# A transformer layer on one core: all five engine orders planned anew, with costs taken from a trace

## The chip, the core and the metric

The kernel runs on one NeuronCore of a Trainium2 chip. The core has a matrix engine (TensorE, PE in the rows), VectorE (DVE), ScalarE (ACT), GpSimd (POOL), SyncE (SP, which here only issues transfers) and 16 DMA engines. The metric is device time in microseconds, from one execution to the next compared by the median. Before the change it is 617.42 us (median of 3 runs, 615.31 to 617.7).

## What is computed

Input is x of shape 4 x 1024 x 128 (four batches of 1024 tokens). One pre-norm layer follows:

```
x = x + attention(layernorm(x), W_attn, W_proj)
x = x + moe(layernorm(x), gate, bias, up, down, shared_up, shared_down)

attention:  q, k, v = x @ W_attn.T            # 16 heads of 8
            K, V = sums of k, v over the sets (0-3), (4-7), ..., (0-7), (8-15), ..., (0-1023)
            logits = q . K over the sets that end at or before t, and q . (sum of k over the set
                     of 4 that t stands in, up to t)
            out = softmax(logits) @ V, then @ W_proj.T
moe:        scores = sigmoid(x @ gate.T); 4 of 8 groups, then 6 of 32 experts per token
            sum over chosen experts of w * relu(x @ up_e.T)^2 @ down_e.T   # inner width 64
            + relu(x @ shared_up.T)^2 @ shared_down.T                       # inner width 256
```

All 32 experts are computed for all tokens and multiplied with a weight that is 0 for those not chosen.

## The kernel before

**Units of work.** Every batch is cut into two windows of 512 tokens. A batch is prepared first: `xload` brings x into tile XP, DVE takes statistics (`stats1`, `aggr1`), POOL the root (`rstd1`), DVE applies them (`apply1`), PE transposes and multiplies (`fill` x, k, q, v, and later l, t, s), ACT takes each result out of PSUM (`evac`), `tails` and `sums` build the sets, `ksplit` and `qsplit` cut k and q into three bf16 parts, `kst`/`qst` store them to DRAM in another layout and `kld`/`qld` load them back into KA and QA. In the first batch half of the stores are ACT's (`kst_odd`, `qst_odd`), and `whigh`/`wlow` split the expert weights.

Then each window goes through four head groups g: `max` (logits for the row maximum, 3 units a group in window 0 and 8 in window 1, lines 955 and 961), `red` (DVE, line 1173, the maximum of a unit), `mfin`, `split`, `mT`, `mcopy`, `rows` (the maxima are brought into extra rows of QA by SP, line 639), `exp` (logits again, 3 or 7 units a group, lines 978 and 983), `expa` (ACT, line 824, the exponential), `pv` (line 1000). After a window: `oevac`, `oT`, `ocopy`, `den`, `ao`, `aT`, `aTe`, `proj`, `x1`, a second norm (`stats2` to `apply2`), `xT`, `xhe`, `xle`, `logits`, the choice of experts on DVE (`sco` to `weights`), `cT`, and `cst`, which stores the weights. Last, 18 expert units per window: `up` (line 1053), `relu` and `sq` on ACT, `bc` (SP fetches the weights, broadcast), `had` (POOL, line 732), `dn` (line 1066). After 18 of them `fin` and `yst` end the window. There are 4 x 36 = 144 expert units, 176 `max` units, 160 `exp` units and 96 `pv` units; in the orders, `dn.2.24` is the `dn` of batch 2, unit 24.

**What sets the order.** Each engine runs through a list of units, written out by `plan()` while the program is built. It is a list scheduler: `work()` gives each unit an engine, a duration and what it stands behind; within a kind the units keep their order; between kinds the unit with the earliest due time goes first, out of those that could start within `AHEAD` of the first. Due times come from `STARTUP`, `PERIOD`, `OFF`, `UNIT_T` and a shift for each kind (`SHIFT`). Nothing of this runs on the chip: there, each engine just takes its list in order and waits on semaphores.

**Banks and tilings.** `max`, `exp` and `fill` take a pair of the six PSUM banks of `ring`, so at most three of them are under way; other kinds take one of the last two banks. PE works in three tilings: `max` and `exp` use 64 rows (two matmuls side by side), `pv` uses 32 columns, all else 128 x 128. The plan charges `SWITCH` for each change of tiling and, among the due times, `STAY` against leaving the present one:

## Time and profile before

| | |
|---|---|
| median of 3 runs | 617.42 us (615.31 to 617.7) |
| span of the profiled execution | 616.0 us |
| PE busy | 556.2 us, 90% |
| DVE busy | 391.3 us, 64% |
| ACT busy | 371.6 us, 60% |
| POOL busy | 282.5 us, 46% |
| mean granted TensorE clock | 0.944 |

The span runs from the first to the last instruction. It is the profiled execution's own time as far as the records go; the runs time a little more around it. Busy time of PE counts a matmul until its modelled end, so that neighbours overlap; the distance from one unit's start to the next one's start is the better measure of what a unit costs, and the chain of waits gives it for units on the chain.

### The profile page before, as it was taken

To read this page: it belongs to the slowest core of one execution; us is meant where nothing else is said; L and a number is where in the kernel's file an instruction comes from. 1 tells how busy PE (TensorE), PEld (TensorE's weight loads), DVE (VectorE), ACT (ScalarE), POOL (GpSimd) and SP (SyncE) were. 2 spreads that over 40 slices of the span, in tenths; PEclk is the share of its full clock that TensorE was granted. 3 is DMA by queue.
4 is the path that set the end of the run, shared out by engine and by line. 5 is a ranking of instruction groups with operands and counts; after the bars stand their busy time and mean duration, and the time that the engine had idled before them with its cause. 6 is when DMAs were issued, how large, how long until landed. Compare 5 with 4: busy or idle time off the path is not lost.

```text
span 616.0 us, 12273 instructions
## 1 busy us (share of the span) xinstructions
PE 556.2 (90%) x4460; PEld 358.7 (58%) x4460; DVE 391.3 (64%) x935; ACT 371.6 (60%) x536; POOL 282.5 (46%) x403
## 2 busy tenths in 40 slices
PE   7246788998899999999999999999899999999997
PEld 6033233354556555566776555666765665688896
DVE  3829967677797857847678758645678776036400
ACT  1310346773646567858655857657566769865674
POOL 2500302731735248355643547444635334366575
PEclk9755679998899999999999999899999999999999
DMA  6683000084532212775342214836322222233452
GB/s 141 181 210 82 2 4 3 14 193 153 129 88 88 75 36 78 183 209 126 90 124 66 72 35 122 190 122 141 117 74 74 79 65 67 78 118 101 124 182 92
DMA packets 49344, 63.56 MB, mean 103 GB/s; under 512 B 8484, under 2 KB 30788, under 8 KB 48004
## 3 DMA queue, kind: packets, MB, share of 16 engines
q1 hardware_dynamic: 47988, 61.60, 36.7%
q10 hardware_dynamic: 1296, 1.18, 0.6%
q8 instruction: 35, 0.57, 0.4%
q14 instruction: 25, 0.20, 0.1%
HBM read 50.31 MB, written 12.06 MB: 101 GB/s over the span
## 4 chain that ended last, share of the span: by engine, by line
PE 59%; DVE 23%; DMA 6%; issue 3%; ACT 3%; POOL 3%; SPq 1%; ACTq 0%; POOLq 0%; DVEq 0%
PE sums_ps L1066 16%; PE ring L1053 12%; PE sums_ps L1000 10%; DVE MXR L1173 7%; PE ring L983 4%; PE ring L961 4%; DVE XN L1121 2%; DMA QA<-q_parts 2%; PE ring L978 2%; ACT PT L824 2%; PE ring L955 2%; PE ring L1007 2%; PE ring L921 2%; PE ring L1035 1%; DMA q_parts<-Qparts 1%
## 5 line engine op out<-in xcount | busy, mean ns | idle before, releaser
L1173 DVE TENSOR_REDUCE MXR<-ring 128x4 f32<-128x1024 f32 (+2 forms) x192 | 175.3, 950 | 75.3 <-PE ring L961 73.1
L732 POOL TENSOR_TENSOR H<-RV,WB 128x512 f32<-128x512 f32 x128 | 162.3, 1279 | 121.8 <-ACT RV L835 114.4
L824 ACT ACTIVATE PT<-ring 128x1024 f32<-128x1024 f32 x160 | 158.7, 1025 | 85.5 <-PE ring L983 84.1
L1066 PE MATMUL sums_ps<-wdown,H 128*128 128x128 f32 x1152 | 155.8, 283 | 0.4 <-POOL H L732 0.3
L1066 PEld LDWEIGHTS sums_ps<-wdown,H 128*128 128x128 f32 x1152 | 141.8, 193 | 21.7 <-issue 14.7
L891 ACT ACTIVATE RV<-ring 128x512 f32<-128x512 f32 x144 | 84.9, 593 | 67.6 <-PE ring L1053 66.9
L1000 PE MATMUL sums_ps<-PT,VA 128*32 128x512 f32 (+1 forms) x768 | 88.7, 553 | 0.1
L835 ACT ACTIVATE RV<-RV 128x512 f32<-128x512 f32 x128 | 80.0, 629 | 2.6
L1053 PE MATMUL ring<-XH,WUH 128*128 128x512 f32 x144 | 67.1, 466 | 0.7 <-ACT RV L891 0.3
L961 PE MATMUL ring<-KA,QA 51*128 51x256 bf16 (+7 forms) x512 | 62.8, 311 | 0.0
L983 PE MATMUL ring<-QA,KA 54*128 54x512 bf16 (+1 forms) x384 | 60.4, 350 | 1.1 <-ACT PT L824 0.6
L1053 PE MATMUL ring<-XH,WUL 128*128 128x512 f32 x144 | 57.3, 398 | 0.0
L1053 PE MATMUL ring<-XL,WUH 128*128 128x512 f32 x144 | 57.2, 397 | 0.0
L955 PE MATMUL ring<-KS,QS 64*128 64x64 bf16 (+1 forms) x384 | 39.0, 214 | 19.9 <-DMA QA<-q_parts 9.2
L721 POOL TENSOR_TENSOR MS<-MALL,zeros 128x16 bf16<-128x16 f32 x32 | 7.9, 247 | 96.5 <-DVE MALL L1184 92.5
L955 PEld LDWEIGHTS ring<-KS,QS 64*128 64x128 bf16 x384 | 17.5, 97 | 53.8 <-issue 24.8
L1000 PEld LDWEIGHTS sums_ps<-PT,VA 128*32 128x32 f32 x768 | 17.2, 110 | 32.6 <-issue 25.5
L978 PE MATMUL ring<-QS,KS 64*128 64x256 bf16 (+1 forms) x192 | 31.0, 319 | 5.6 <-DMA QA<-MB 2.0
L1053 PEld LDWEIGHTS ring<-XH,WUH 128*128 128x128 f32 x144 | 27.5, 191 | 12.6 <-issue 6.4
L1053 PEld LDWEIGHTS ring<-XH,WUL 128*128 128x128 f32 x144 | 27.2, 189 | 6.5
L983 PEld LDWEIGHTS ring<-QA,KA 54*128 54x128 bf16 x384 | 18.7, 96 | 21.0 <-issue 8.4
L555 POOL TENSOR_TENSOR TAIL<-TAIL 128x256 f32<-128x256 f32 x21 | 15.6, 743 | 32.4 <-ACT TAIL L800 31.3
(128 smaller groups left out, 676.2 us busy)
## 6 DMA issues: line engine op xcount, KB each, us to landing
WB<-combine SPq DMA_DIRECT2D x256, 128.0 KB, 2.9
QA<-q_parts SPq DMA_DIRECT2D x16, 384.0 KB, 6.1
KA<-k_parts SPq DMA_DIRECT2D x8, 384.0 KB, 6.2
q_parts<-Qparts SPq DMA_DIRECT2D x14, 192.0 KB, 5.6
XP<-in_x_dram SPq DMA_DIRECT2D x4, 512.0 KB, 5.4
X<-in_x_dram SPq DMA_DIRECT2D x4, 512.0 KB, 4.4
out_dram<-OT SPq DMA_DIRECT2D x8, 256.0 KB, 2.3
q_parts<-Qparts SPq DMA_DIRECT2D x14, 128.0 KB, 4.8
```

Of the source, the lines that this page charges most:

```text
L732: pool.tensor_tensor(H[:, m % NHB, :], RV[:, m % NRV, :], WB[:, r % NWB, :], ALU.mult).then_inc(s_had, 1)
L824: act.activation(dst, src, ACT.Exp, scale=SCALE).then_inc(s_expa, 1)
L835: act.activation(rv, rv, ACT.Square).then_inc(s_sq, 1)
L891: act.activation(RV[:, m % NRV, :], single("up", b, *k), ACT.Relu).then_inc(s_relu, 1)
L955: pe.matmul(own, QS[r:r + HALF, P * (i % 2):P * (i % 2) + P], mask, start=(k == 0), stop=False, skip_group_check=True)
L961: ins = pe.matmul(bank[:, e, at + ns * q:at + ns * q + ns], QA[r:r + K_RAW, w, h, P * (i % WT):P * (i % WT) + P], KA[r:r + K_RAW, b % 2, h ...
L978: pe.matmul(bank[:, e, 0:2 * P * nq].rearrange("p (q t) -> p q t", q=nq), KS[r:r + HALF, :], mask, start=True, stop=False, skip_group_chec ...
L983: ins = pe.matmul(bank[:, e, nt * q:nt * q + nt], KA[r:r + K_SUB, b % 2, h, P * c:P * c + P], QA[r:r + K_SUB, w, h, t0 - WIN * w:t0 - WIN ...
L1000: ins = pe.matmul(opsum[32 * h:32 * h + 32, t0 - WIN * w:t0 - WIN * w + nt], VA[:, v0:v0 + 32], PT[:, pv_number(b, w, g, k) % NPT, h, 0:nt ...
L1053: ins = pe.matmul(single("up", b, u), wa[:, P * j:P * j + P], xa[:, window(w)], start=(k == 0), stop=(k == 2))
L1066: ins = pe.matmul(dsum[:, P * i:P * i + P], H[:, m % NHB, P * i:P * i + P], wdown[:, CHUNKS[n], :], start=(n == 0 and i == 0), stop=(n == ...
L1173: ins = dve.reduce_max(MXR[:, g, i, :, q0:q0 + nq], pair("max", b, w, g, n)[:, :, at:at + ns * nq].rearrange("p e (q s) -> p e q s", s=ns) ...
```

## The change

The builder of the instructions is the same, line for line (it stands 28 lines further down). What changes is `work()` and `plan()`, and so the order of the units on all five engines. The same 836 PE units, 427 DVE units, 536 ACT units, 210 POOL units and 208 SP units are issued, with the same operands. The PSUM bank of a unit and the waits for banks follow from the new order.

```diff
-LAG = {"pe": 0.24, "dve": 0.16, "act": 0.17, "pool": 0.15, "sp": 0.15}
+LAG = {"pe": 0.30, "dve": 0.13, "act": 0.14, "pool": 0.19, "sp": 0.03}
+LAG_OF = {"exp": 0.23, "max": 0.24, "pv": 0.14, "mT": 0.21, "up": 0.27, "expa": 0.20, "oevac": 0.20, "et": 0.23, "split": 0.12, "rstd2": 0.0,
+          "x1": 0.19, "sco": 0.11}
...
-                    put(("max", b, w, g, n), "pe", max(0.11 + 0.06 * (len(parts) - 1), cols * 0.42e-3) + 0.027 * len(parts), (("kld", b), 5.0),
-                        (("qld", b, w), 5.0))
-                    put(("red", b, w, g, n), "dve", 0.08 * len(parts) + 2 * cols * 1.04e-3, (("max", b, w, g, n), 0.24))
+                    put(("max", b, w, g, n), "pe", MAX_US[w][n], (("kld", b), 6.2), (("qld", b, w), 6.0))
+                    put(("red", b, w, g, n), "dve", 0.07 * len(parts) - 0.01 + 2 * cols * 1.04e-3, ("max", b, w, g, n))
...
-SWITCH, STAY = 0.09, 18.4
-STARTUP, PERIOD = 40.0, 101.1
+TURNS = ("aT", "cT", "oT", "xT", "fill")
+COLD = (22.0, 73.0)
+STAY, FEW, WAIT = {128: 52.3, 64: 36.3, 32: 37.4}, 8.3, 0.0
+
+
+def turnover(rows, kind):
+
+    to = ROWS_OF.get(kind, 128)
+    if to == rows or kind == "mT":
+        return 0.0
+    if to == 64:
+        return 0.11 if rows == 128 else 0.08
+    if to == 32:
+        return 0.165
+    return (0.14 if kind in TURNS else 0.19) - (0.02 if rows == 32 else 0.0)
+
+
+STARTUP, PERIOD = 22.0, 95.0
...
 def due(name):
 
-    return stage_due(name) + SHIFT.get(name[0], 0.0)
+    kind, b = name[:2]
+    return stage_due(name) + SHIFT.get(kind, 0.0) + (FIRST.get(kind, 0.0) if b == 0 else LAST.get(kind, 0.0) if b == B - 1 else 0.0)
...
-            if eng == "pe" and ROWS_OF.get(kind, 128) != rows:
-                at += SWITCH
+            if eng == "pe":
+                at += turnover(rows, kind)
...
-            late = lambda x: STAY if eng == "pe" and ROWS_OF.get(x[2][0], 128) != rows else 0.0
-            pick = min((x for x in c if x[0] <= limit + (SWITCH if eng == "pe" else 0.0)), key=lambda x: (x[1] + late(x), x[0], str(x[2])))
+            if eng == "pe":
+                pairs_free = sum(all(unit is None or (FREED_BY[unit[0]],) + unit[1:] in done and done[(FREED_BY[unit[0]],) + unit[1:]] < limit + 0.3
+                                     for unit in held[j:j + 2]) for j in range(0, NBANK, 2))
+                same = lambda x: ROWS_OF.get(x[2][0], 128) == rows
+                late = lambda x: 0.0 if same(x) else STAY[ROWS_OF.get(x[2][0], 128)] + (FEW * (3 - pairs_free) if x[2][0] in ("max", "exp") else 0.0)
+                pick = min((x for x in c if x[0] <= limit + (WAIT if same(x) else 0.2)), key=lambda x: (x[1] + late(x), x[0]))
+            else:
+                pick = min((x for x in c if x[0] <= limit), key=lambda x: (x[1], x[0]))
...
-        done[name] = free[eng] = at + W[name][1]
+        done[name] = free[eng] = at + W[name][1] * (2.0 if eng == "pe" and COLD[0] < at < COLD[1] else 1.0)
```

`SHIFT` grows from 21 kinds to all kinds, and `FIRST` and `LAST` are new tables of the same form for batch 0 and batch 3. Three places show what comes of it.

**SP, first batch, from the end of the constants to the second window's q.** Before (`k_parts<-Kparts` is a piece of `kst`, `q_parts<-Qparts` of `qst`; `KA<-` and `QA<-q_parts` are `kld` and `qld`; `X<-` is `xres`, `XP<-` is `xload`):

```order
L585 DMA X<-in_x_dram 128x8x128
L549 DMA k_parts<-Kparts 64x3x512
L549 DMA k_parts<-Kparts 64x2x512
L549 DMA k_parts<-Kparts 64x512
L618 DMA KA<-k_parts 48x4096 x2
L549 DMA q_parts<-Qparts 64x3x512
L549 DMA q_parts<-Qparts 64x2x512
L549 DMA q_parts<-Qparts 64x512
L633 DMA QA<-q_parts 48x4096 x2
L549 DMA q_parts<-Qparts 64x3x512
L549 DMA q_parts<-Qparts 64x2x512
L549 DMA q_parts<-Qparts 64x512
```

After:

```order
L577 DMA k_parts<-Kparts 64x3x512
L577 DMA k_parts<-Kparts 64x2x512
L577 DMA k_parts<-Kparts 64x512
L577 DMA q_parts<-Qparts 64x3x512
L577 DMA q_parts<-Qparts 64x2x512
L577 DMA q_parts<-Qparts 64x512
L646 DMA KA<-k_parts 48x4096 x2
L577 DMA q_parts<-Qparts 64x3x512
L577 DMA q_parts<-Qparts 64x2x512
L577 DMA q_parts<-Qparts 64x512
L613 DMA XP<-in_x_dram 128x8x128
L661 DMA QA<-q_parts 48x4096 x4
```

`X<-in_x_dram` has moved from here to the very first place on SP, ahead of the first batch's `XP<-in_x_dram`. The first window's q parts are stored before k is loaded back, and the first `qld` stands behind the second window's stores and the next batch's `XP` load, where it stood ahead of both.

**PE, first batch, around the first `exp` units.** Before (`L955` with `L961` is a `max` unit, `L978` with `L983` an `exp` unit):

```order
L955 MATMUL ring<-KS,QS 128x64 x2
L961 MATMUL ring<-KA,QA 128x384 x2
L955 MATMUL ring<-KS,QS 128x64 x2
L961 MATMUL ring<-KA,QA 128x384 x2
L955 MATMUL ring<-KS,QS 128x64 x2
L961 MATMUL ring<-KA,QA 128x320 x2
L955 MATMUL ring<-KS,QS 128x64 x2
L961 MATMUL ring<-KA,QA 128x320 x2
L955 MATMUL ring<-KS,QS 128x64 x2
L961 MATMUL ring<-KA,QA 128x512 x2
L978 MATMUL ring<-QS,KS 128x256 x2
```

After:

```order
L1112 MATMUL ring<-identb,MS 48x128
L1006 MATMUL ring<-QS,KS 128x256 x2
L1011 MATMUL ring<-QA,KA 128x512 x2
L1006 MATMUL ring<-QS,KS 128x256 x2
L1011 MATMUL ring<-QA,KA 128x512 x2
L983 MATMUL ring<-KS,QS 128x64 x2
L989 MATMUL ring<-KA,QA 128x448 x2
L983 MATMUL ring<-KS,QS 128x64 x2
L989 MATMUL ring<-KA,QA 128x448 x2
L1112 MATMUL ring<-identb,MS 48x128
L1006 MATMUL ring<-QS,KS 128x512 x2
```

The first `exp` unit (`L978`, now `L1006`) stood behind 21 of the batch's 44 `max` units and stands behind 14 now; from there on `max` and `exp` alternate. `L1084`, now `L1112`, is `mT`.

**PE, last batch, `max` units of window 1.** Before:

```order
L955 MATMUL ring<-KS,QS 128x64 x2
L961 MATMUL ring<-KA,QA 128x384 x2
L1066 MATMUL sums_ps<-wdown,H 128x128 x4
L955 MATMUL ring<-KS,QS 128x64 x2
L961 MATMUL ring<-KA,QA 128x320 x2
L978 MATMUL ring<-QS,KS 128x256 x2
L983 MATMUL ring<-QA,KA 128x512 x2
L1000 MATMUL sums_ps<-PT,VA 32x256 x4
L955 MATMUL ring<-KS,QS 128x64 x2
L961 MATMUL ring<-KA,QA 128x320 x2
L1066 MATMUL sums_ps<-wdown,H 128x128 x4
```

After:

```order
L1094 MATMUL sums_ps<-wdown,H 128x128 x4
L983 MATMUL ring<-KS,QS 128x64 x2
L989 MATMUL ring<-KA,QA 128x448 x2
L983 MATMUL ring<-KS,QS 128x64 x2
L989 MATMUL ring<-KA,QA 128x384 x2
L983 MATMUL ring<-KS,QS 128x64 x2
L989 MATMUL ring<-KA,QA 128x384 x2
L1028 MATMUL sums_ps<-PT,VA 32x256 x4
L1028 MATMUL sums_ps<-PT,VA 32x512 x4
L1028 MATMUL sums_ps<-PT,VA 32x256 x4
L1011 MATMUL ring<-QA,KA 128x512 x4
L1094 MATMUL sums_ps<-wdown,H 128x128 x8
```

Three `max` units (with 384, 320 and 320 columns) stood apart, with a `dn` (`L1066`) behind the first and the last. Now three (448, 384, 384) stand together, three `pv` units follow, and two `dn` are together behind them. Over the whole list the tiling changes 355 times before and 297 times after (into 128: 122 and 79; into 64: 157 and 136; into 32: 76 and 82).

Counted over the lists: between the first `max` of batch 1 and the last of batch 3 stand 96 `up` and 92 `dn` before, 73 and 74 after; the 132 `max` units there are the same. Behind the last `exp` unit stood 43 `dn`, and 62 stand there now. From `fill` k of batch 1 to that batch's first `max` unit there were 41 PE units and are 57, among them 1 `up` before and 5 after.

## Rows read from the trace of the kernel before

**Rows 1.** Part 1 of the page: busy us, share of the span, instructions.

```profile
PE 556.2 (90%) x4460; PEld 358.7 (58%) x4460; DVE 391.3 (64%) x935; ACT 371.6 (60%) x536; POOL 282.5 (46%) x403
```

**Rows 2.** Engine times by stretch: us, busy by engine, clock, DMA share, GB/s.

```profile
0.00:46.00 46.00, 21.39 (x108) 17.41 (x108) 20.58 (x53) 9.61 (x11) 13.44 (x26) 0.74 0.72 176
46.00:115.00 69.00, 55.82 (x461) 21.24 (x461) 53.83 (x104) 27.31 (x31) 15.85 (x40) 0.75 0.10 21
...
141.00:507.00 366.00, 355.67 (x2964) 227.76 (x2959) 265.53 (x605) 238.25 (x348) 179.08 (x258) 0.99 0.38 104
507.00:616.00 109.00, 102.23 (x751) 81.94 (x750) 32.90 (x111) 76.63 (x122) 61.77 (x54) 1.00 0.33 108
```

**Rows 3.** Chain of waits, 298 to 309: start us, us, what.

```profile
299.37 1.09 PE sums_ps L1066 x8
300.46 1.39 PE ring L1053 x6
301.86 0.89 PE sums_ps L1066 x8
```

**Rows 4.** Chain of waits, 0 to 60 (stats, mv: the norm's statistics).

```profile
0.74 4.18 DMA XP<-in_x_dram
...
5.02 0.89 DVE stats L1109 x4
...
6.04 0.89 DVE stats L1109 x4
...
7.06 0.66 DVE mv L1114 x8
...
33.47 6.05 DMA q_parts<-Qparts
...
39.89 6.11 DMA QA<-q_parts
```

**Rows 5.** Timeline of SP, 0 to 50: start us, us, transfer issued.

```profile
11.11 7.11 SPq L585 DMA_DIRECT2D X<-in_x_dram  x1
...
39.54 0.77 SPq L633 DMA_DIRECT2D QA<-q_parts  x2
40.36 1.94 SPq L549 DMA_DIRECT2D q_parts<-Qparts  x3
42.41 1.11 SPq L585 DMA_DIRECT2D XP<-in_x_dram  x1
```

**Rows 6.** Engine times in three stretches of 2 us.

```profile
2.00:4.00 2.00, 2.00 (x12) 2.00 (x11) 0.00 (x0) 0.23 (x2) 1.03 (x5) 1.00 0.79 233
44.00:46.00 2.00, 0.00 (x0) 0.00 (x0) 0.00 (x0) 0.00 (x0) 0.00 (x0) 0.50 0.90 215
138.00:140.00 2.00, 0.00 (x0) 0.00 (x0) 0.00 (x0) 1.08 (x2) 0.00 (x0) 1.00 0.91 246
```

**Rows 7.** Waits of PE, 46 to 115: total us, times, longest.

```profile
PE ring L955 <- DVE MXR L1173: 6.6, 17, 0.6
...
PE ring L978 <- DVE MXR L1173: 1.4, 4, 0.6
```

**Rows 8.** Chain of waits, 135 to 165.

```profile
131.58 9.11 DMA QA<-q_parts
...
155.47 5.35 DMA QA<-MB
```

**Rows 9.** Waits of PE, 141 to 507.

```profile
PE ring L1007 <- DVE XN L1121: 3.1, 3, 1.6
...
PE ring L955 <- DVE MXR L1173: 1.8, 2, 1.3
...
PE ring L978 <- DVE MXR L1173: 0.4, 1, 0.4
```

**Rows 10.** Waits of PE, 507 to 616.

```profile
PE ring L1007 <- DVE XN L1121: 1.5, 1, 1.5
PE ring L1041 <- POOL WSEL L782: 1.3, 1, 1.3
```

More of the change, by code:

```diff
@@ L146, in put @@
     def put(name, eng, us, *behind):
-        W[name] = (eng, us, [x if len(x) == 2 and isinstance(x[0], tuple) else (x, LAG[kind_engine(x[0])]) for x in behind if x])
+        lag = LAG_OF.get(name[0], LAG[eng])
+        W[name] = (eng, us, [x if len(x) == 2 and isinstance(x[0], tuple) else (x, lag) for x in behind if x])
     def later(x, us):
@@ L226, in work @@
[L226 to L228 removed]
+                     ("x1", "dve", 0.6), ("stats2", "dve", 0.76), ("aggr2", "dve", 0.75),
@@ L262 @@
 ROWS_OF = {"max": 64, "exp": 64, "pv": 32}
[L263 to L268 removed]
+MAX_US = [[0.28, 0.23, 0.29], [0.25, 0.25, 0.22, 0.22, 0.20, 0.20, 0.17, 0.17]]
@@ new lines @@
+TURNS = ("aT", "cT", "oT", "xT", "fill")
[11 more added lines that the diff above has]
+STARTUP, PERIOD = 22.0, 95.0
+OFF = {"att0": -46.4, "att1": 35.9, "ffn0": 135.9, "ffn1": 176.5, "prep": -25.6, "post": 24.9, "max": -47.3}
@@ new lines @@
+UNIT_T = 3.21
+AHEAD = {"pe": 0.0, "act": 0.3, "dve": 0.08, "pool": 0.11, "sp": 0.83}
+SHIFT = {"xload": -94.5, "stats1": 136.0, "aggr1": -62.2, "rstd1": 193.8, "apply1": 107.4, "fill": -14.7, "evac": -0.4, "tails": 85.8, "sums": 78.9, "ksplit": 24.7, "qsplit": 112.7, "prod": 0.2, "kst": 5.3, "kst_odd": 49.6, "kld": 14.2, "qst": -75.2, "qst_odd": 87.5, "qld": -59.4, "xres": -180.3, "max": -1.9, "red": -23.7, "mfin": -13.9, "split": 62.1, "mT": -54.5, "mcopy": -80.3, "rows": -50.1, "exp": -14.2, "expa": -28.8, "pv": 41.8, "oevac": 274.2, "oT": -34.9, "ocopy": 54.3, "td": 42.5, "et": 17.2, "tailw": 89.7, "den": 173.0, "ao": -90.6, "aT": -86.2, "aTe": -161.5, "proj": -6.8, "x1": 45.4, "stats2": -31.5, "aggr2": -35.7, "rstd2": -57.9, "apply2": 14.0, "xT": -25.0, "xhe": -116.6, "xle": -52.0, "logits": -31.2, "sco": 72.2, "score": -0.7, "pairs": -49.4, "groups": 82.8, "groups2": 31.4, "experts": 164.2, "experts2": 180.9, "weights": 176.6, "parts": 40.2, "cT": -123.7, "cTe": -62.9, "cst": 167.2, "up": -24.3, "relu": -19.9, "sq": -16.3, "dn": 40.7, "bc": -93.6, "had": -123.4, "fin": -12.5, "yst": -152.9, "whigh": 138.6, "wlow": -47.2}
@@ new lines @@
+FIRST = {"xload": -23.6, "stats1": 36.5, "aggr1": 153.8, "rstd1": 128.9, "apply1": 53.0, "fill": 50.1, "evac": 79.5, "tails": -52.2, "sums": -17.5, "ksplit": -8.0, "qsplit": 111.1, "prod": -6.1, "kst": 40.9, "kld": -132.1, "qst": -36.0, "qld": -79.1, "xres": 9.4, "max": -13.2, "red": -49.3, "mfin": -117.5, "split": 91.2, "mT": -96.6, "mcopy": -59.6, "rows": -36.2, "exp": -12.4, "expa": 87.0, "pv": 44.4, "oevac": 65.7, "oT": -18.5, "ocopy": -40.8, "td": 78.0, "et": -93.8, "tailw": -30.8, "den": -126.0, "ao": 195.5, "aT": 26.9, "aTe": -110.8, "proj": -41.4, "x1": -28.5, "stats2": -64.5, "aggr2": 25.8, "rstd2": -30.7, "apply2": 40.2, "xT": -19.6, "xhe": -9.8, "xle": 105.5, "logits": 49.5, "sco": 81.4, "score": 208.4, "pairs": 74.7, "groups": 77.6, "groups2": -42.2, "experts": -75.9, "experts2": -177.3, "weights": 12.5, "parts": 176.0, "cT": -138.1, "cTe": 88.7, "cst": 4.1, "up": -14.0, "relu": -89.7, "sq": 111.9, "dn": -21.2, "bc": -59.0, "had": 88.0, "fin": 88.8, "yst": -35.9}
@@ new lines @@
+LAST = {"xload": 80.9, "stats1": -29.8, "aggr1": 45.2, "rstd1": 44.1, "apply1": -51.2, "fill": -14.7, "evac": -80.1, "tails": -92.4, "sums": 46.0, "ksplit": 115.3, "qsplit": -53.7, "prod": -111.3, "kst": -51.1, "kld": -86.5, "qst": 93.7, "qld": -145.3, "xres": -35.5, "max": 4.0, "red": 9.7, "mfin": -50.1, "split": -78.3, "mT": -51.7, "mcopy": -81.6, "rows": -63.1, "exp": -8.6, "expa": 89.0, "pv": -8.4, "oevac": 80.5, "oT": 39.6, "ocopy": -22.5, "td": -60.0, "et": 184.2, "tailw": -164.3, "den": -228.7, "ao": -129.8, "aT": -36.2, "aTe": -100.9, "proj": -46.4, "x1": 43.6, "stats2": -105.5, "aggr2": -60.0, "rstd2": -104.9, "apply2": 15.1, "xT": -102.6, "xhe": -22.3, "xle": -85.3, "logits": 26.9, "sco": -29.3, "score": 251.8, "pairs": 111.7, "groups": 31.7, "groups2": 32.8, "experts": -111.6, "experts2": 154.6, "weights": 26.6, "parts": 24.2, "cT": -191.6, "cTe": -22.5, "cst": 4.4, "up": -144.3, "relu": 180.2, "sq": -89.0, "dn": 67.2, "bc": 56.1, "had": -74.3, "fin": -129.0, "yst": 51.8}
```

75 lines of the change are left out of this document (35 added, 40 removed).

## Prediction

> **What bounds the kernel now.** I read the page's busy shares first. PE is busy for 556.2 of 616.0 us, no other engine for more than 391.3 [rows 1]. An average over stages says little, so next come the engine times by stretch [rows 2], and the reader is to see four stages. In 0 to 46 PE is busy 21.39 us of 46: the first batch is prepared in one chain from a load through DVE and PE to DRAM and back. In 46 to 115 nothing but the first batch's attention can run: PE 55.82 of 69 at a mean clock of 0.75, DVE 53.83 of 69. In 141 to 507 PE is busy 355.67 of 366 at clock 0.99, DVE 265.53. In 507 to 616 it is 102.23 of 109. So over three quarters of the time PE has work without a break, and only three things can shorten that part: cheaper work on PE, less of it in the wrong place, or fewer waits, of which there are few. PE's waits for VectorE's maxima are 8.0 us in the 69 us of the second stage (6.6 and 1.4 [rows 7]) and 2.2 us in the 366 us of the third [rows 9].
>
> The set of units is the same after the change, so every microsecond must come from a change of tiling, a wait, or the clock. Six terms follow, each against the profiled execution's 616.0 us.
>
> **1. Changes of tiling: -8.6 us.** The chain of waits shows what one costs. A `dn` between `exp` work and an `up` took 1.09 us from its start to the next one's, a `dn` that follows an `up` and is followed by 128-row work 0.89 [rows 3]: 0.20 for an excursion into 128 rows, without what it costs the unit before. Entries into 128 rows go from 122 to 79, 43 fewer: 43 x 0.20 = 8.6. The lower bound takes 0.10 for each single change, half of that: 58 fewer changes make 5.8. The upper takes 0.29 an excursion, as if the unit before paid half again (43 x 0.29 = 12.5); the six more entries into 32 are within this. I take 8.6, the row's own number. The Trainium skill has a rule here: "Changing tiling mode (not just tile) drains the TensorE" (TensorEngine Tiling (Array Packing), Key Properties), and TensorE: Matmul & The Clock Gate (Part 2, Step-by-step) puts a drain at 128 cycles. As an estimate from those pages, 58 drains at 2.4 GHz are 58 x 0.053 = 3.1 us; the row's 0.20 for two changes is about twice that, so the measurement decides.
>
> **2. The first `max` unit comes later: +5.5 us.** Two moves on SP lie on the opening chain. X is now issued ahead of XP. XP landed 4.18 us after its issue [rows 4], when it was first; X was issued last, at 11.11 [rows 5]. X has the same 512 KB, and in 2 to 4 us the queues moved 233 GB/s [rows 6], so 2.2 us of transfer, and 0.3 for the issue, stand ahead of it: +2.5. Bounds: 0.4, if both share and XP hardly suffers, and 4.2, the whole of another load. Everything up to the first `max` hangs on it. Second, the first `qld` was issued at 39.54, right when q had landed (6.05 us after the last piece's issue), and itself landed 6.11 us later [rows 4]; the second window's stores (40.36) and the next XP (42.41) stood behind it [rows 5] and now stand ahead. These are 384 KB and 512 KB; at the 215 GB/s of 44 to 46 [rows 6] they are 4.2 us. The part issued while q is still in flight is hidden: I take +3, bounds 0 and 4.2. The first `kst` waits behind `wlow` now, but k lands before q in both. The Trainium skill says of one SDMA engine that "descriptors are consumed in ring order" (DMA: Bandwidth & Descriptors, Queues, rings and completion order); by it alone both moves cost their full transfer, and the sum would be 1.2 higher (4.2 in place of 3). No row here shows two such loads in the other order.
>
> **3. The first batch's attention is shorter: -8.6 us.** The statistics of batch 1 (for batch 0 they took 0.89, 0.89 and 0.66 us [rows 4]) ran between reductions; now they stand ahead of the first one, where DVE waits anyway: -2.4. Then `exp` starts behind 14 `max` units instead of 21, and `exp` and `max` alternate. In 46 to 115 DVE idled 69 - 53.83 = 15.2 us and ACT was busy 27.31 [rows 2]; DVE was saturated before the exponentials began and idle after. Alternating them should take back part of the 15.2; I take 6.2, less than half, since PE is at the low clock for a part of the stretch and its own 55.82 us leave 13. Bounds 0 and 12.6. In all 8.6, bounds 2.4 and 15.
>
> **4. Handover to batch 1: -3.5 us.** `qld` of batch 1 took 9.11 us to land and PE had nothing to do in 138 to 140; then the maxima's rows took 5.35 [rows 8], behind a load that waited for an `exp`. Now 57 PE units stand between `fill` k and the first `max` instead of 41, four of them `up`: about 8 us more cover (4 x 0.70 for `up`, half of the 1.39 of two [rows 3], the rest attention). Against it, `kld` is queued behind the second window's stores, the q load and XP, some 5 us later. Net 3, and 0.5 for the rows. Bounds: -8, all waits of this place, and +3 if the k load is the later one.
>
> **5. Waits of PE behind the post-attention chain: -3 us.** PE waited 3.1 us for the normalised x in the third stage [rows 9], 1.5 in the last, and 1.3 there for the expert weights [rows 10]. In the third stage the distance to `xT` grows by many units, except for batch 0. Behind `proj.3.1` stand the same four `up` and four `dn` as before, so the last 1.5 and the 1.3 stay. Bounds 0 and -4.4.
>
> **6. Denser attention: +5 us.** This is what the change pays. Between the first `max` of batch 1 and the last of batch 3 stand 23 `up` and 18 `dn` fewer (23 x 0.70 + 18 x 0.89 = 32 us) and 62 changes fewer; they move behind, where nothing competes. The stretch shrinks from 366 to about 325 us (366 less 32, less 62 changes at half of 0.29) and the 132 reductions do not. DVE's 265.53 us are 73% of 366 and would be up to 82% of 325 (less, since the routing of two windows leaves the stretch too). At 73% PE lost 2.2 us to DVE. At 53.83 / 69 = 78% in the second stage it lost 8.0, which is 0.116 per us; over 325 us that is 38. So the bounds are 0 and +35. I stay near the third stage's row, because there too three bank pairs and expert units lay between reductions, while the second stage had no expert work at all: +5. ACT (238.25 of 366) and POOL (179.08) have room.
>
> Sum: -8.6 + 5.5 - 8.6 - 3.5 - 3 + 5 = -13.2, so 602.8. The runs' median is 1.4 above the span (617.4 against 616.0), and I add it: 604.
>
> **Rivals.**
>
> *A, the full gain.* The terms 3 and 4 reach further, since work that was in the wrong place at the low clock now keeps PE warm: term 3 at -14, term 4 at -6, term 6 at +1. 616.0 - 8.6 + 5.5 - 14 - 6 - 3 + 1 = 590.9, with 1.4 about 592. For it: 13 us of PE and 15 of DVE idle in the second stage at once. Against it: the opening chain stays serial.
>
> *B, VectorE becomes the bound (slower).* Place: batches 1 to 3, where `max` and `exp` share three bank pairs. If PE loses to DVE even half of the second stage's rate (0.058 per us x 325 = 19, less the 2.2 of now: +17), and the opening gives back only the moved statistics (term 3 at -2.4) and term 2 stands, then 616.0 - 8.6 + 5.5 - 2.4 - 1.5 - 3 + 17 = 623, with 1.4 about 624. It decides from about 13 us of new waits in the middle if the opening also yields little. For it: 82% is above the share at which PE did wait. Against it: the 2.2 us at 73%, over 366 us.
>
> *C, the change does little.* Tilings are saved (-8.6), the opening loses 5.5 and regains 2.4, the middle takes 5, the rest stays: 616.0 - 8.6 + 5.5 - 2.4 + 5 = 615.5, about 617. For it: each of the terms 3 to 5 rests on dues that fit one set of durations, and an order fixed in advance pays for every duration that is off.
>
> *D, the trade of 1 against 2 only.* A milder C, with half of terms 3 to 5: about 612 (616.0 - 8.6 + 5.5 - 7.5 + 5, and 1.4).
>
> **How the numbers follow.** The forecast (598 to 608) gets 0.45, A 0.20, D 0.12, C 0.09, B 0.14. A measurement of this kernel can tell about 0.5% from no change, 3.1 us: faster is below 614.3, slower above 620.5. Forecast, A and D lie on the faster side: 0.77. C is 0.09 for no change, B is 0.14 for slower. The range from 590 to 618 leaves out B and the far end of A. The forecast's own range is 597 to 610.
>
> **What would show it.** Term 1: entries such as 1.09 for a `dn` get rarer, and the third stage's PE work from the first `max` of batch 1 to the last of batch 3 takes about 325 us. Term 2: the first reduction begins at 51 to 53 us instead of 47. Term 3: the last reduction of batch 0 ends about 112 us in, less than 62 us behind the first. Term 4: PE's wait for QA or KA near 135 us falls under 3 us. Term 5: the waits of PE for the normalised x are 1.5 to 2 us in all. Term 6: the sum of PE's waits for the maxima in the middle stays under 8 us; 15 or more speaks for B. From the last `exp` unit on, with 62 `dn` left instead of 43, PE should need 0.89 + 0.70 a unit, without a break. The prediction is wrong at its root if PE's idle time in the middle, not the tilings, decides the difference.

## The result, and the profile after

| | before | after |
|---|---|---|
| median | 616.45 us (615.31 to 617.7, 4 runs) | 630.86 us (627.16 to 633.49, 4 runs) |
| ratio, 95% interval | | 1.0206 [1.0168, 1.0245] |
| profiled execution, span | 616.0 us | 630.1 us |
| changes of PE's tiling | 355 | 297 |

The change made the kernel 2.1% slower. I had forecast 2% faster, and the result lies outside my range. (The 617.42 us at the start of this document is the median of three of these four runs of before.) This is the page of the changed kernel, part 1 (compare [rows 1]): busy us, share of the span, instructions.

```profile
PE 556.2 (88%) x4460; PEld 366.3 (58%) x4460; DVE 385.9 (61%) x935; ACT 372.4 (59%) x536; POOL 279.0 (44%) x403
```

No engine has noticeably more to do (ACT 0.8 us more, DVE and POOL less, PE the same). The same stretches as in [rows 2]:

```profile
0.00:46.00 46.00, 25.26 (x108) 19.84 (x108) 20.85 (x53) 9.49 (x11) 13.46 (x26) 0.73 0.62 157
46.00:115.00 69.00, 50.74 (x451) 20.64 (x455) 54.72 (x105) 26.96 (x30) 19.48 (x50) 0.76 0.15 34
141.00:507.00 366.00, 341.53 (x2914) 211.74 (x2912) 253.26 (x592) 238.14 (x336) 164.91 (x251) 0.98 0.36 97
507.00:616.00 109.00, 104.11 (x738) 90.75 (x739) 38.43 (x122) 72.73 (x125) 67.26 (x56) 1.00 0.40 124
```

In the 366 us of the third stretch PE had been busy for 355.67 us and idle for 10; it is now idle for 24. PE's waits in this stretch, to be held against [rows 9] (total us, times, longest):

```profile
PE ring L1081 <- DVE MB L1312: 4.1, 3, 2.0
PE ring L1112 <- POOL MS L752: 3.8, 1, 3.8
PE ring L1006 <- DMA QA<-MB: 2.6, 1, 2.6
PE ring L1035 <- DVE XN L1149: 2.4, 2, 1.7
PE ring L983 <- DVE MXR L1201: 2.4, 3, 1.5
...
PE ring L983 <- DMA KA<-k_parts: 1.5, 1, 1.5
PE ring L1011 <- DVE MXR L1201: 1.3, 4, 0.4
```

The first three are links of one kind of chain, at five different places: the maxima go through VectorE, GpSimd (MS), PE (`mT`), VectorE (MB) and a transfer (QA<-MB) before `exp` may start. These links cost 2.0 us before and cost 10.5 now.

To compare stages I take PE's own work out. From the trace of before I fitted, for each kind of unit, its start-to-start time where nothing waits at full clock, and a price for each change of tiling (0.10 to 0.17 us). Summed over the lists this is PE's own work. What is left of a stretch is waiting or low clock; I call it the rest. It can be read to about 1 us, and it is only as good as the fitted prices.

| stage | before: length, rest | after: length, rest |
|---|---|---|
| to the first `max` | 46.2, 37.4 | 54.8, 46.0 |
| to the last `max` of batch 0 | 68.4, 29.9 | 61.1, 21.5 |
| to the first `max` of batch 1 | 26.1, 6.1 | 30.4, 6.6 |
| to the last `max` of batch 3 ("the middle") | 366.5, 18.3 | 340.0, 36.1 |
| to the end | 105.1, 2.1 | 140.1, 5.9 |

Own work fell from 518.6 to 510.3 us, the rest grew from 93.8 to 116.1.

**The opening.** The chain of waits of the changed kernel, 0 to 62 (start us, us, what), beside [rows 4]:

```profile
1.24 5.44 DMA XP<-in_x_dram
...
13.70 1.74 PE ring L944 x8
...
16.61 3.80 PE ring L949 x4
...
37.41 6.28 DMA q_parts<-Qparts
...
44.47 10.12 DMA QA<-q_parts
...
54.84 0.29 PE ring L983 x2
```

XP landed at 6.68 instead of 4.92: 1.8 us later. But `fill` k took 3.80 us, and in the kernel before this (the same view):

```profile
11.95 1.08 PE ring L916 x8
...
14.20 2.00 PE ring L921 x4
```

The engine times in 15 to 18 us, before and then after, give the reason: a clock of 1.00 before, 0.50 (1.2 of 2.4 GHz) after.

```profile
15.00:18.00 3.00, 3.00 (x8) 1.33 (x7) 0.69 (x2) 1.09 (x2) 0.00 (x0) 1.00 0.98 330
```

```profile
15.00:18.00 3.00, 1.82 (x5) 0.87 (x4) 0.00 (x0) 1.02 (x1) 0.00 (x0) 0.50 0.90 311
```

The two runs that exchange only moves on SP (below) show it both ways: with XP first again, `fill` k runs at clock 1.00, and in the kernel before with X put first it runs at 0.50. How the delay lowers the clock is not shown. PE stood still for 2.82 us ahead of `fill` x instead of 2.21, but in the fastest kernel below it stood still for 2.09 us there, less than in the kernel before, and its clock was 0.50 all the same. PE's timeline in the kernel before, the changed one and that fastest one, and the fastest one's engine times in 12 to 14 us:

```profile
11.95 1.06 PE L916 MATMUL ring<-ident,XP 128*128 128x128 f32 x8 [2.21 <-DVE XP L1121]
```

```profile
13.70 1.73 PE L944 MATMUL ring<-ident,XP 128*128 128x128 f32 x8 [2.82 <-DVE XP L1149]
```

```profile
12.04 1.94 PE L1002 MATMUL ring<-ident,XP 128*128 128x128 f32 x8 [2.09 <-DVE XP L1207]
```

```profile
12.00:14.00 2.00, 1.94 (x8) 1.57 (x8) 0.00 (x0) 0.00 (x0) 0.00 (x0) 0.50 0.99 123
```

The q parts then left 3.9 us later than before, and the load back, behind two stores and XP, took 10.12 us instead of 6.11.

**The handover to batch 1.** The chain, 135 to 168, beside [rows 8]: the k load is now the late one, and the maxima's rows take as long as they did.

```profile
134.96 11.33 DMA KA<-k_parts
...
159.80 4.90 DMA QA<-MB
```

**The longest wait of the middle.** The chain, 245 to 262, then SP's and POOL's timelines:

```profile
241.65 5.27 DMA combine<-CT
...
250.68 2.93 DMA WB<-combine
...
257.54 0.27 PE ring L1112
```

```profile
241.18 0.43 SPq L613 DMA_DIRECT2D XP<-in_x_dram  x1
241.65 0.67 SPq L709 DMA_DIRECT2D combine<-CT  x1
246.94 9.67 SPq L678 DMA_DIRECT2D WB<-combine  x14
```

```profile
251.66 3.73 POOL L760 TENSOR_TENSOR H<-RV,WB 128x512 f32<-128x512 f32 x3 [10.45 <-DMA WB<-combine]
255.34 1.02 POOL L806 TENSOR_TENSOR rstd<-var,neg_half 128x4 f32<-128x4 f32 x1
```

The store of the expert weights, issued just behind a 512 KB load, took 5.27 us (1.6 in the calm, from issue to landing, as for the 5.27). GpSimd stood still for 10.45 us in front of a product that needs them, with `split` behind it in its list, and PE stood in front of `mT`. Four lists fixed in advance met at a transfer that came late.

### The profile page after: what moved, and what is told of

Read it like the earlier page. It is cut to its first block, busy times and chain, and to the rows that moved or that the text cites. A ratio compares the mean times of both kernels' runs of the same rounds, so it can differ in the third digit from the quotient of the medians.

```text
span 630.1 us, 12274 instructions
## 1 busy us (share of the span) xinstructions
PE 556.2 (88%) x4460; PEld 366.3 (58%) x4460; DVE 385.9 (61%) x935; ACT 372.4 (59%) x536; POOL 279.0 (44%) x403
## 3 DMA queue, kind: packets, MB, share of 16 engines
q1 hardware_dynamic: 47988, 61.60, 36.1%
## 4 chain that ended last, share of the span: by engine, by line
PE 50%; DVE 23%; DMA 9%; issue 5%; SPq 4%; ACT 4%; POOL 2%; ACTq 1%; POOLq 0%; DVEq 0%
PE sums_ps L1094 14%; PE ring L1081 11%; DVE MXR L1201 8%; PE sums_ps L1028 6%; PE ring L1011 3%; PE ring L989 3%; PE ring L949 3%; DVE XN L1149 2%; DMA QA<-MB 2%; ACT PT L852 2%; PE ring L1006 2%; DMA KA<-k_parts 2%; SPq L577 2%; PE ring L1035 2%; PE ring L1063 2%
## 5 line engine op out<-in xcount | busy, mean ns | idle before, releaser
L1094 PE MATMUL sums_ps<-wdown,H 128*128 128x128 f32 x1152 | 153.4, 281 | 0.4 <-POOL H L760 0.3
L1094 PEld LDWEIGHTS sums_ps<-wdown,H 128*128 128x128 f32 x1152 | 144.5, 194 | 15.2 <-issue 7.3
L863 ACT ACTIVATE RV<-RV 128x512 f32<-128x512 f32 x128 | 78.3, 628 | 2.2
L983 PE MATMUL ring<-KS,QS 64*128 64x64 bf16 (+1 forms) x384 | 38.8, 213 | 19.4 <-DMA QA<-q_parts 9.9
L983 PEld LDWEIGHTS ring<-KS,QS 64*128 64x128 bf16 x384 | 18.2, 97 | 57.6 <-issue 20.2
L1334 DVE TENSOR_TENSOR OT<-sums_ps,X 128x512 f32<-128x512 f32 x8 | 5.5, 690 | 63.7 <-PE sums_ps L1094 63.7
L1006 PE MATMUL ring<-QS,KS 64*128 64x256 bf16 (+1 forms) x192 | 31.4, 323 | 7.4 <-DVE MXR L1201 2.9
L1081 PEld LDWEIGHTS ring<-XH,WUH 128*128 128x128 f32 x144 | 27.6, 192 | 13.0 <-DVE MB L1312 5.0
```

The source lines that it names most:

```text
L863: act.activation(rv, rv, ACT.Square).then_inc(s_sq, 1)
L983: pe.matmul(own, QS[r:r + HALF, P * (i % 2):P * (i % 2) + P], mask, start=(k == 0), stop=False, skip_group_check=True)
L1006: pe.matmul(bank[:, e, 0:2 * P * nq].rearrange("p (q t) -> p q t", q=nq), KS[r:r + HALF, :], mask, start=True, stop=False, skip_group_chec ...
L1081: ins = pe.matmul(single("up", b, u), wa[:, P * j:P * j + P], xa[:, window(w)], start=(k == 0), stop=(k == 2))
L1094: ins = pe.matmul(dsum[:, P * i:P * i + P], H[:, m % NHB, P * i:P * i + P], wdown[:, CHUNKS[n], :], start=(n == 0 and i == 0), stop=(n == ...
```

## The experiments

Each ratio is against runs of the kernel before taken beside it; the changed kernel's is 1.0206 [1.0168, 1.0245]. Two ratios whose intervals overlap widely are not told apart. A rest is read from one execution, a ratio from four or more.

**Undoing parts of the change.** `move(list, unit, before)` moves one unit in one list.

```diff
+move(ORDER["sp"], ("xload", 0), ("xres", 0))        # after, opening of SP
+move(ORDER["sp"], ("kld", 0), ("qst", 0, 0))
+move(ORDER["sp"], ("qld", 0, 0), ("qst", 0, 1))
```

> The changed kernel with three moves on SP in batch 0 undone: XP is issued ahead of X, k is loaded back ahead of the first q store, and the first window's q is loaded ahead of the second window's stores. All other orders are those of the changed kernel. If the opening chain is what the change pays for, the first max unit starts at 47 to 49 us instead of 54.8, and the end moves with it: 623 to 625 us against the changed kernel's 630.9. The rival says that the first batch's attention has its own limit (DVE, low clock) and that what is gained at the start is waited for later: first max at 47 to 49 all the same, but 628 to 631 at the end.

Measured: 1.0171 [1.0089, 1.0253]. The first `max` came at 49.6 us, 5.2 earlier and 0.6 behind the latest I had expected, but the first batch's attention then took 64.3 us instead of 61.1. The middle's rest stayed (36.4). The median, 629.12 us, lies where the rival had it (628 to 631), and the ratio is not told apart from the changed kernel's, so this run does not show how much of the 2.1% is the opening's.

The reverse, the same SP moves made in the kernel before:

```diff
+move(ORDER["sp"], ("xres", 0), ("xload", 0))        # before, opening of SP
+# kld.0 behind qst.0.0; qld.0.0 behind qst.0.1 and xload.1
```

> The kernel before with only the two moves on SP that my term 2 is about: X ahead of the first XP, and the first loads back of k and q behind the stores, and q's behind XP of batch 1, as in the changed kernel. PE's list and the lists of VectorE, ScalarE and GpSimd are those of the kernel before. By my term 2: first max 5.5 us later, 621 to 623 us. By the trace of the changed kernel, where it came 8.6 us later: 8 us or more later, and 622 to 626 us if nothing of it is regained before batch 1; under 619 us if the handover to batch 1, which waits for a q load issued at its own time, absorbs it.

Measured: 1.0093 [1.0059, 1.0126], 5.7 us of 616. The first `max` came at 54.9, 8.7 us later; 2.2 us were regained in the first batch. So the two moves by themselves make the first `max` as late as in the changed kernel: term 2's mechanism is shown, and its size at the first `max` was put too low (5.5 against 8.7). That the part which reaches the end, 5.7, is near my 5.5 is luck, since the term had nothing in it about regaining 3 us.

```diff
 # e2: after, with the due times, AHEAD and STAY of before
 # e3: after, with work(), LAG, prices and COLD of before, and the new due times
```

> The new durations, waits, tiling prices and opening clock, but the due times, the look-ahead and the single price for leaving a tiling (18.4) of the kernel before. PE then changes its tiling 302 times (355 before, 297 after). Theory: the newly searched due times are what costs, since they leave no room at the handoffs; then this kernel keeps the saving of 53 changes at 0.145 us, 7.7 us, and little else: 606 to 613 us. Rival: the new durations themselves give an order that does not fit the chip; then 622 or more.

> The other half: the newly searched due times and leaving rule with the durations, waits and single price of a tiling change of the kernel before (no low clock in the plan). 332 changes of tiling. If the due times cost time whatever durations they are used with, 625 to 640 us. If it needs both, or the new durations alone do it, 612 to 620.

Measured: 1.068 [1.0612, 1.0748] and 1.0208 [1.0141, 1.0274]. The old due times do badly with the new costs (middle's rest 52.6), as the rival had it. The new ones do as badly with the old costs as with their own, as their theory had it, though the middle's rest is smaller (27.3) and other stages lose it. Each half of the change by itself costs as much as both or more, so the two runs don't single out one of them.

**Mending single places of the changed kernel.**

```diff
+move(ORDER["pool"], ("split", 2, 0, 0), ("had", 0, 20))
+move(ORDER["sp"], ("cst", 0, 1), ("xload", 3))
```

> The changed kernel with two units moved: on POOL the split of batch 2, window 0, group 0 stands ahead of had.0.20 (which waited 10.4 us for its weights), and on SP the store of the expert weights of batch 0, window 1 stands ahead of the 512 KB XP load (it took 5.3 us to land behind it). If PE's 3.8 us at 253 us were a wait for POOL that waited for a transfer, they vanish and the end moves by 2 to 4 us: 627 to 629. If they only stood in for a wait that comes next (had.0.20 itself is needed by dn.0.20, the unit right behind), the wait moves on by one unit and the time stays within 1 us of 630.9.

Measured: 1.0282 [1.0217, 1.0348], 634.57 us, slower than either reading had it. The store landed after 3.80 us instead of 5.27. The wait for MS at 253 us is gone, and PE's waits in 235 to 280 now begin with a longer one, for a reduction (middle's rest 37.0):

```profile
PE ring L993 <- DVE MXR L1211: 4.3, 1, 4.3
```

```diff
-MB = sb("MB", [3 * G * WT, P], bf16)
+MB = sb("MB", [3 * G * WT, 2, P], bf16)      # a copy and a semaphore each
```

> The changed kernel with two copies of tile MB and a semaphore for each, so that mcopy of one head group need not wait until the rows of the one before have landed. The profile charges 4.7 us of PE's waits in the middle to DVE MB (at units that need mT's bank). Theory 2a (these waits are lost time): 4 to 5 us faster than the changed kernel, 1.4% above the kernel before. Theory 2b (the lists are so tight that the next link is late then, as with the two moves tried before): less than 2 us, 1.8% to 2.1% above it.

Measured: 1.0143 [1.0078, 1.0208], about 4 us better by the medians, which is 2a's size; but the four runs span 622 to 631 us, and the interval reaches to the changed kernel's ratio, so 2b's "less than 2 us" is not excluded. In the profiled execution, the fastest of the four, PE's waits for MB in 141 to 507 are 0.7 us instead of 4.1, and the middle's rest is 27.6. That the wait of `mcopy` for the rows before it was lost time is likely, not shown. The plan of either kernel has no such term; it only lets `mT` stand 1.8 us behind the issue of those rows.

```diff
-                    sp.dma_start(WB[HALF * e:HALF * e + HALF, n % NWB, :],
-                                 Cd[r // 16, 2 * (r % 16) + e].partition_broadcast(HALF)).then_inc(s_wb[n % NWB], 16)
+                    sp.dma_start(WB[HALF * e:HALF * e + HALF, n % NWB, 0:WIN // 4],
+                                 Cd[r // 16, 2 * (r % 16) + e, 0:WIN // 4].partition_broadcast(HALF)).then_inc(s_wb[n % NWB], 16)
```

> The changed kernel, but each of the 128 broadcasts of expert weights moves the first 128 of its 512 columns (the tile is set to zero at the start, so that the other weights are 0; all instructions are the same otherwise). Three quarters of the largest stream of transfers go. Theory D (transfers that land late behind other transfers feed the new waits: cst.0.1 took 5.3 us, the first rows of batch 1 5 us and more): the wait of 3.8 us at 253 us and the one of 2.6 us at 161 us shrink to under 1 us, and the kernel gains 5 to 9 us, 622 to 626 us. Against it (landings are only the last link, the lists decide): under 3 us, 628 us or more.

Measured: 1.0176 [1.0128, 1.0223]; the middle's rest is 32.5. That is some 2 us by the medians, which is not clear of noise; 629.53 us lies where the reading against theory D had it. The wait for MS at 253 us is still 3.3 us, and the store before it took 5.20. So the kernel's largest stream isn't what makes the transfers late that matter.

**VectorE's load.** The same edit in the changed kernel and in the kernel before:

```diff
-                                         pair("max", b, w, g, n)[:, :, at:at + ns * nq].rearrange("p e (q s) -> p e q s", s=ns), AX.X)
+                                         pair("max", b, w, g, n)[:, :, at:at + ns * nq].rearrange("p e (q s) -> p e q s", s=ns)[:, :, :, 0:ns // 2], AX.X)
```

> The changed kernel, but each of VectorE's 176 reductions reads only the first half of every set of columns (the maxima are those of half the logits; all else is as in the changed kernel). VectorE's work in the middle falls well below what it was before the change. Theory 1 (VectorE is too densely loaded in the shortened middle, as rival B has it): the 18.6 us of new waits between the first max of batch 1 and the last of batch 3 go, and this kernel gains at least 15 us more over the changed kernel than the same edit gains in the kernel before: below 608 us. Theory 2 (the waits are those of the order itself: a row of handovers through VectorE, GpSimd, SyncE and a transfer, placed without slack): the first batch gains some 6 us, as in the kernel before, the middle 5 at most: 617 to 624 us.

> The kernel before, with the same edit: VectorE reduces half the columns. Its waits for maxima were 8.0 us in the first batch and 2.2 us in the middle, so both theories expect 606 to 612 us here. It is the measure for the other kernel: theory 1 wants a gain there that is larger by 15 us or more, theory 2 one that is the same within 5 us.

Measured: 1.0025 [0.9998, 1.0052] and 0.9783 [0.9755, 0.9811]: 1.8% and 2.2% gained, the same within the intervals. Theory 1, and my rival B with it, is out. PE's waits in 141 to 507 of the changed kernel with half reductions:

```profile
PE ring L1081 <- DVE MB L1312: 4.1, 3, 2.3
PE ring L1112 <- POOL MS L752: 3.9, 1, 3.9
PE ring L1006 <- DMA QA<-MB: 2.7, 1, 2.7
```

The three waits of the maxima's chain are the old ones within 0.1 us, though VectorE does half the reducing. The middle's rest did fall by 8.3 us, against 4.1 in the kernel before, so some 4 of the 18 new microseconds may be VectorE's load.

**GpSimd's load.** Again in both kernels:

```diff
-                pool.tensor_tensor(H[:, m % NHB, :], RV[:, m % NRV, :], WB[:, r % NWB, :], ALU.mult).then_inc(s_had, 1)
+                pool.tensor_tensor(H[:, m % NHB, 0:64], RV[:, m % NRV, 0:64], WB[:, r % NWB, 0:64], ALU.mult).then_inc(s_had, 1)
```

> The changed kernel, but GpSimd's 128 products with the expert weights take the first 64 of 512 columns (the rest of the tile stays 0 or old); all lists are the same. GpSimd is then free early, and VectorE hardly ever waits for it. Theory G (the new waits come from GpSimd: its queue, in which split stood behind three products at 250 us, and the waits of VectorE for its operations): the kernel gains at least 10 us more than the kernel before does by the same edit, and the wait of 3.8 us at 253 us is gone. Theory 2 (the lists are short of slack at many places, each with another partner): the two gains differ by less than 6 us.

> The kernel before with the same short products: the control. VectorE was held up by GpSimd for 48 us in it and for 43 us in the changed kernel, mostly off the path, so both theories expect a gain of 3 to 12 us here.

Measured: 0.9913 [0.987, 0.9955] and 0.9812 [0.977, 0.9853]: 2.9% and 1.9% gained. The gains differ by 6.5 us with an interval of some 4 us either way, which lies between the two theories; in the middle the kernel before gained more (rest 18.3 to 5.8) than the changed one (36.1 to 26.4). PE still waited 2.7 us for MS, at the same place (252.7 us), where theory G had the wait gone. PE's waits in 141 to 507:

```profile
PE ring L1114 <- POOL MS L752: 2.7, 1, 2.7
```

So GpSimd costs both kernels time, and it is not shown to be what sets them apart.

**PE's list or the other four.** A rule makes the four side lists: the unit goes first whose result PE's list needs earliest.

```diff
+ORDER, PLACE, BEHIND, _ = sides(ORDER["pe"])
```

> PE's list of the changed kernel word for word; the lists of VectorE, ScalarE, GpSimd and SyncE are made anew by a plain rule: of the units that can start, the one goes first whose result is needed earliest by PE's list, with longer landings assumed for transfers (2.5 us for the maxima's rows, 3.5 for the expert weights' store, 4.0 for their broadcast). Theory 3 (the searched side lists bring the waits, PE's list is sound): the middle's new waits shrink from 18.6 to under 8 us and the time falls to 612 to 620 us. Theory 2 (PE's list itself leaves no slack): within 8 us of the changed kernel, 624 to 640 us, and not below the next kernel.

> PE's list of the kernel before word for word; the four other lists by the same rule as in the run before this one, so that the two differ in PE's list alone. Theory 2: within 10 us of the kernel before (610 to 627 us), and not slower than the kernel with the changed PE list. Theory 3: slower than the kernel with the changed PE list by 8 us or more, since that has 58 changes of tiling fewer.

Measured: 1.0294 [1.0265, 1.0322] and 1.0303 [1.0236, 1.037]. The rule is poor, so the absolute times say little, but with side lists of one make PE's two lists take the same time. Both theories had a part wrong: the kernel before lost 3% by it, the changed one under 1%. So what the kernel before had was, in the main, side lists that fit its PE list. PE's changed list isn't cleared by this: it holds some 8 us less of PE's own work, and at equal times it waits that much more.

**The same search with other costs.** The last four kernels have all five lists written out. A search moves single units and keeps what a replay of the lists finds shorter.

```diff
-ORDER, PLACE, BEHIND, NUMBER, _, _ = plan()
+ORDER, PLACE, BEHIND = read_lists()      # LISTS and SPOTS written out
```

> A new order: all five lists are written out. They were found by moving single units in the lists of the kernel before, each move scored by replaying the lists with durations and handovers read from the traces of the kernels run so far, with two things the plan of either kernel has no term for: transfers that share the queues land later, and mcopy waits for the rows before it. All durations of VectorE and GpSimd and all landings were disturbed at random, and an order had to be good under several draws. It has 325 changes of tiling, and 22 max units ahead of the first exp. Theory C (the search was sound and its costs were not): with true costs an order faster than both exists and is found: under 605 us. Rival (a fixed order found by search always promises what the chip does not give, whatever its costs): 612 us or more.

Measured: 606.28 us, 0.9794 [0.9747, 0.9842]. Faster than both, and 1 us above theory C's mark.

> The same search as in the run with measured costs (same start, the lists of the kernel before; same moves, same number of them, same seed), but each move is scored with the costs that the changed kernel's plan has: its durations, delays, price for a change of tiling and slow clock between 22 and 73 us, nothing disturbed. 308 changes of tiling. Theory C (the costs are what fails): no faster than the kernel before, 614 to 630 us. Rival (the due times are what fails, and a search free of them finds a good order with these costs too): within 5 us of the run with measured costs, 603 to 611 us.

Measured: 632.58 us, 1.0213 [1.0163, 1.0263], 2.6 us above theory C's range and far from the rival's. With the plan's own costs the same search, from the same start, lands where the change did, and its middle has the same kind of waits (rest 41.7; PE's waits in 141 to 507):

```profile
PE ring L1064 <- DMA QA<-MB: 3.5, 1, 3.5
PE ring L1139 <- DVE MB L1370: 3.3, 1, 3.3
...
PE ring L1064 <- DVE MB L1370: 2.5, 1, 2.5
```

The two differ in more than the table: the measured costs were also disturbed at random over four draws, so a part of the 4.2% may be slack that this bought.

> The same search again with measured costs and one thing more in the replay, which the run with measured costs brought out: an operation of VectorE with two inputs in SBUF waits until a running operation of GpSimd has ended, and the other way round (the routing's 32-column operations took 0.19 us alone and 1.15 to 1.20 beside GpSimd's product of 1.3 us; pairs of batch 0, window 1, took 5.37 us instead of 1.61). Start: the lists of the kernel before. 344 changes of tiling. Theory C2 (this wait is the largest cost that the first replay lacked; it promised more than the chip gave): under 596 us. Rival (the rest is scatter that no replay holds): 602 us or more.

> The same replay as in the run before this one, searched longer and from the lists of the changed kernel: 323 changes of tiling, 12 max units ahead of the first exp. If theory C2 holds, this is the fastest of all, 575 to 595 us, though it starts from the lists that were slower; if the order of the changed kernel is itself a poor start, it stays above the run before this one.

Measured: 598.15 us, 0.9682 [0.9635, 0.9729], and 595.46 us, 0.9628 [0.9584, 0.9671]. The first missed its mark of 596 and beat the rival's 602. Its replay differed in more than the expectation says: slower q and k loads and VectorE operation by operation came with the wait, three draws were used for four, and a quarter fewer moves, so the 1.1% over the run with measured costs is not the wait's alone. The second, a longer search out of the changed kernel's lists, missed its range by half a microsecond; it is the fastest by its median, but its interval overlaps the first one's. Its page, part 1, and PE's and the others' busy times in its middle and in the changed kernel's:

```profile
PE 551.2 (93%) x4460; PEld 362.7 (61%) x4460; DVE 370.9 (63%) x935; ACT 369.0 (62%) x536; POOL 272.3 (46%) x403
```

```profile
131.00:452.00 321.00, 315.96 (x2759) 196.37 (x2757) 230.35 (x540) 217.21 (x311) 153.61 (x248) 0.99 0.40 103
```

```profile
146.00:486.00 340.00, 318.39 (x2742) 197.47 (x2742) 234.66 (x525) 218.10 (x307) 154.08 (x239) 0.97 0.35 96
```

This middle is shorter than the changed kernel's by 19 us, holds the same 132 `max` units and a little more of PE's own work (309.7 against 303.9 us), has VectorE at 72% instead of 69%, and its rest is 11.4 us instead of 36.1. Dense attention is no fault in itself: this middle is the shortest of the three kernels' and has the smallest rest.

## Why the prediction was wrong

| term | predicted | measured, us |
|---|---|---|
| 1, tilings | -8.6 | -8.3 (own work, by fitted prices) |
| 2, first `max` later | +5.5 | +8.6 |
| 3, first batch's attention | -8.6 | -8.4 |
| 4, handover to batch 1 | -3.5 | +0.5 |
| 5 and 6, waits behind attention, denser attention | +2 | +17.8 in the middle, +3.8 behind it |
| sum | -13.2 | +14.0 (spans: +14.1) |

- Term 1 was right. 58 changes gave 8.3 us, 0.14 each, so the row of `dn` beside `exp` and `up` was a fair price. The 8.3 is a sum of prices over the new list, not a time that one row shows; the same kind of fit made on the changed kernel's trace alone gives about 9. The estimate from the drain that the Trainium skill puts at 128 cycles (TensorE: Matmul & The Clock Gate, Part 2, Step-by-step) was 3.1 us, and these traces have more than twice that.
- Term 2 had the right mechanism and was mis-sized. X cost 1.8 us of landing, not 2.5, but some 2 more because PE's clock had fallen before `fill` k, which my sum had no term for; the q load's 4.0 us were near the upper bound of 4.2, not 3. The Trainium skill's rule that one SDMA engine takes its descriptors in ring order (DMA: Bandwidth & Descriptors, Queues, rings and completion order) gave 4.2 for the q load, and the trace is nearer to it than to my 3. In the kernel before, this step cost 5.7 us at the end.
- Term 3 came out in size: the first batch's `max` units span 61.1 us (forecast: under 62). But part of this is luck. A late opening shortens this stage by itself, by 2.2 us in the kernel before with the changed opening, and with the old opening put back it takes 64.3 us, 4.1 less than before instead of 7.3. The last `max` starts 1.3 us later than before, and the last reduction ends at 117.8 us, not at the 112 that I had put.
- Term 4 failed. I counted cover by PE units. It hid the q load, and the k load became the late one (11.33 us), as the bound on the slow side (+3) said; PE's own wait for k was 1.5 us, and the rows still cost 2.6.
- Term 5 failed. The normalised x cost 4.4 us in all (4.6 before), the expert weights 3.7 (1.6 before), where I had put 3 us less. These waits end on chains through VectorE and GpSimd, whose lists changed as well. This is the last stretch, 507 to 616, against [rows 10]:

```profile
PE ring L1069 <- POOL WSEL L810: 3.7, 3, 1.4
PE ring L1035 <- DVE XN L1149: 2.0, 2, 1.5
```

- **Term 6 is the step that failed.** "I stay near the third stage's row" looked at one releaser, VectorE's maxima, and there it was right: PE waited 5.2 us for them in the middle (2.4 and 1.3 of them in the rows above), under my mark of 8. I put +5 for the term, and the rest of the middle grew by 17.8. I read the 366 us of the middle as a stretch with slack because PE hardly waited in it. As I read it now, that it waited for nobody was the result of five lists that fit each other. The new lists were made with costs that leave out what the chip does: rows that must land before the next `mcopy`, transfers late behind others, VectorE held up by GpSimd, stretches at the low clock after the first batch. PE then waited for many releasers, 1 to 4 us each, and none of my bounds was built on them. The middle was to take 325 us and took 340, which is what my last sign named: PE's idle time in the middle, not the tilings, decided the difference. The plan of the kernel before leaves out the same things, so the gaps in the costs alone do not set the two apart; that the new lists lean on them harder is my reading, and the search with the plan's costs, 2.1% slow as well, supports it.
- No rival had this mechanism. B came nearest in time (624) with the wrong cause; halved reductions rule it out. C named it in one clause ("an order fixed in advance pays for every duration that is off") and priced it at 5 us.

Shown: the waits and their sizes; that VectorE's load is not the main cause; that the changed opening costs 5.7 us in the kernel before; that a search over the same lists ends 2.1% above the kernel before with the plan's costs and 2.1% below it with measured, disturbed ones. Not shown: how the 17.8 us of the middle divide among the missing costs; whether the MB wait was worth its 4 us; which half of the change does the harm; and how much of the gain of the last searches is the true durations and how much the random disturbance.

## What to carry to other kernels

When every engine runs a fixed list, hardly any waiting in the old profile can be a sign that the lists fit, not that there is slack: price a new set of lists by the chains that cross engines and transfers, not by the busiest engine. Before trusting a search, replay the kernel at hand in its cost model and look at every place where the chip comes later; what the model lacks, the search will lean on. Disturb its durations too, so that no order wins that needs them all to be exact (here measured costs and disturbance came together, and neither was tried alone).

## What the hardware showed that I had not expected

- VectorE's operations stand still beside GpSimd's. In the first search's kernel, VectorE's and then GpSimd's timeline, 178 to 187 us:

```profile
180.97 0.19 DVE L1323 TENSOR_TENSOR wrem<-hi 128x32 f32<-128x32 f32 x1
181.19 1.15 DVE L1324 TENSOR_TENSOR wrem<-hi 128x32 f32<-128x32 f32 x1
182.38 0.19 DVE L1325 TENSOR_TENSOR wrem<-hi 128x32 f32<-128x32 f32 x1
```

```profile
181.00 1.30 POOL L818 TENSOR_TENSOR H<-RV,WB 128x512 f32<-128x512 f32 x1 [0.41 <-ACT RV L921]
```

  An operation of two inputs in SBUF and of the same size takes 0.19 us alone and 1.15 beside the product. Operations with one tensor input do it too: the normalisation's `apply` operations took 0.34 us where GpSimd was idle, and up to 1.44 where it ran. Summed over each operation's excess over its undisturbed time, reductions left out, this is 48 us of VectorE in the kernel before and 43 in the changed one, about half of it in operations with two inputs in SBUF. The Trainium skill (SBUF — State Buffer, Who interferes with whom) says so: the two share a port pair as an exclusive lock, and the loser blocks fully. The trace agrees; reductions out of PSUM beside GpSimd kept their time (1.21 us beside GpSimd and 1.22 alone, for the largest of them).
- A small transfer can land late behind others: the 64 KB store of expert weights took 1.6 us in the calm and 5.27 behind an output store and a 512 KB load, and still 3.80 with that load put behind it; a q load took 6.11 and 10.12 us. So the large load is only a part of it.
- With X ahead of XP the first XP landed 1.8 us later, and PE ran the next `fill` at half the clock (2.00 and 3.80 us). The wait ahead of it doesn't explain this by its length: 2.82 us of idle PE here, 2.21 in the kernel before at full clock, and 2.09 at half clock in the fastest kernel.
